# Three-layer attention block on one core: the second attention's probabilities in two layouts, with new waits and order at the start and around the third layer norm

## The chip, the cores and the metric

The kernel runs on one core of a Trainium2 chip and is written in Bass, with a program of its own for each engine: TensorE (PE; its weight loads are listed as PEld), VectorE (DVE), ScalarE (ACT), GpSimd (POOL) and SyncE (SP, which only issues DMAs here). The engines run side by side and meet at semaphores: `engine.wait_ge(sem, n)` holds an engine until the count is n, `.then_inc(sem, 1)` raises it. Each engine takes its instructions in the order in which they are written. The metric is the time on the device in microseconds (us). Of the kernel before there are three timed runs, 743.19, 739.35 and 742.94 us (median 742.94), and one profiled execution of 739.54 us.

## The reference

Everything is float32. Three residual layers act on x (4 batches of 128 rows, 512 wide, 16 heads of 32).

```
x = x + cross_attention(layernorm(x), ctx)   # ctx (4, 2048, 512); softmax over the 16*4 head-batch axis
x = x + relative_attention(layernorm(x))     # logits and values also take tables of relative distances:
#   attn = softmax((q.k + q.Ek[rel] + k.Eq[rel] + Eq[rel].Ek[rel]) / sqrt(32))
#   out[b,h,l] = sum_m attn[b,h,l,m] v[b,h,m] + sum_m attn[b,h,l,m] Ev[rel[l,m]]
x = x + third_attention(layernorm(x))        # normalised queries, learned offset and temperature,
#   softmax, gates by a softmax with top 3 of 15, output projection
```

The last sum of the second layer is the *table product* of this text. Ev[rel[l,m]] depends on the query row l, so each of the 128 rows l has a matrix (128 keys x 32) of its own, and is multiplied with the 64 probability columns (16 heads x 4 batches) of that row.

## The kernel before

**Start.** SP loads x in one DMA of 1 MB (`load(x_res[:], x_rows, "x_in")`), then Wq, the bias columns, Wk, the first context tile and the rest. DVE waits for x, takes mean and variance of batch after batch (L1329, L1331), ACT takes the square root (L894; an activation table is loaded first) and DVE writes the normalised rows (L1338). PE transposes them (L363), with two small products between the batches whose result is not used (`keep_warm`, L524). ACT splits the transposed rows and Wq into a high part (casts, L967 and L957); the low part comes from DVE (L1355, L1359). The query projection (L538, L543) starts when all four high parts of x and both halves of Wq's are there.

**First attention** (to about 546 us): 16 context tiles, a loop that this change does not touch.

**Second attention** (about 565 to 660 us), in four head groups u of 4 heads. `relative(n)` makes the table terms of the logits in 16 pieces, which SP stores to DRAM (`rel_scratch`) and loads back with shifted rows (`rel_load`); `logits(u)` (PE, L655 and L660) adds the products; `add2(u)` (DVE, L1512) adds the other table term; `softmax2(u)` takes the maximum and subtracts it (L1516, L1518); `exp2(u)` is on ACT (L1093), for u = 3 in 16 activations of one head and batch each (L1099, released in two halves by `softmax2_last`, L1523 to L1529). `total2(u)` sums over the keys (DVE, L1533). `attention_t(u)` transposes the probabilities on PE (L681) into PSUM; `at_copy(u)` (ACT, L1113) brings them into `blocks`, for u = 2 DVE does it (L1562). `blocks` holds, for a key in each partition, [u, batch, head, query row l]. `values2(b)` projects the values (L391), `attend2(u)` multiplies probabilities and values (L715) for one head group. The table product (L745) is 128 products of `ev_rel[:, l, :]` (128 keys x 32, the stationary operand) with

```
blocks[:, :, :, l].rearrange("p (u b) j -> p b u j", u=C)     # 64 columns, 512 bytes apart
```

in four PSUM banks of 8 x 4; between bank 0 and bank 1, PE transposes the attended values (`attended_t`, L733), and DVE scales them and adds x (L1573, L1575). An fp32 product with a plain weight shows as two records in the trace, so the table product has 256 records.

**Third layer norm** (about 655 to 675 us): DVE transposes the table product (L1581), POOL scales it by the inverse sums (L1311), PE adds it to PSUM (`table_values`, L762), DVE, ACT and PE do the norm and its transposes, `queries3(b)` projects (L391).

What sets the order is the text of each engine's program alone: no scheduler and no planner is in between. PSUM has eight banks (`ps[:, n, :]`), and who uses which is given by OUT_BANKS, THIRD_BANKS, LN_BANKS and the bank arguments.

Of the kernel before, what the change touches and what calls it, by code (L numbers as in the profile page):

```python
# [12 lines left out]
P = 128  # L13
B = 4
# [23 lines left out]
def program(nc, a, out):  # L38

    with ExitStack() as ctx:  # L40
# [102 lines left out]
        THIRD_BANKS = (7, 5, 6, 4)  # L143
# [13 lines left out]
        def ln_bank(k, b):  # L157
            return (4 + b, LN_BANKS[b], (4, 5, 6, 4)[b])[k]
# [70 lines left out]
        def probs_t(u):  # L229
            return blocks[:, u * B:(u + 1) * B]  # L230

        names = """x_in wq_in wk_in wv_in cols_in bv_in bo_in tab_in ctx_in_0 ctx_in_1 ctx_hi ctx_lo wq_split xq_split wkv_hi wkv_lo wraw_in wodd_in wsplit_hi wsplit_lo wo_lo wq2_lo
# [5 lines left out]
            ev_in kf_evac kr_evac qr_evac q2_psum q2_evac k2_psum v2_psum v2_evac rel_psum rq_evac rk_evac  # L238
# [3 lines left out]
            at_psum at_done at_dve av2 av2_evac av2_t av2_mul av2_done ev2 ev_t ev_mul x2_psum x2_done  # L242
# [3 lines left out]
            lg3_psum max3 sub3 exp3 sum3 rinv3 rexp3 rb_psum ot3_done at3_psum at3_done av3 ot3_evac ot3_hi ot3_lo  # L246
            g_psum g_bias g_max g_sub g_exp g_top g_steps y_psum fin_done out_done""".split()
# [15 lines left out]
        def _(sp):  # L263
# [3 lines left out]
            x_rows = a["x"].rearrange("b q e -> q b e")  # L267
            load(x_res[:], x_rows, "x_in")
# [82 lines left out]
        def _(pe):  # L351
# [284 lines left out]
            def values2(b, bank):  # L636
                if b == 0:
                    weight_ready(3)
                if b == 0:
                    pe.wait_ge(s["rk_evac"], 2 * C)  # L640
                else:
                    pe.wait_ge(s["at_done"], (2, B + 1, B + 2)[b - 1])
# [21 lines left out]
            def attention_t(u):  # L664
                base = 0 if u < 2 else 4
# [4 lines left out]
                elif u == 2:  # L670
                    pe.wait_ge(s["lg_done"], C + 1)
                for b in range(B):
                    if u == 1:
                        pe.wait_ge(s["at_done"], b + 1)
                        if b == 1:
                            pe.wait_ge(s["v2_evac"], 2)
                    if u == C - 1:
                        pe.wait_ge(s["at_dve"], b + 1)
# [26 lines left out]
            values2(2, 0)  # L705
            values2(3, 1)
            logits(3)

            def attend2(hg):
                for b in range(B):  # L710
                    if hg == C - 1:
                        pe.wait_ge(s["at_done"], 2 * B + b + 1)
# [24 lines left out]
            pe.wait_ge(s["ev_in"], 16)  # L737
            for bank in range(4):
# [1028 lines left out]
```

## Time and profile before

| | |
|---|---|
| timed runs, us | 743.19, 739.35, 742.94 (median 742.94) |
| profiled execution | 739.54 us; span from the first to the last instruction 737.3 us |
| PE | 710.5 us busy (96% of the span), granted clock 0.998 on the mean |
| DVE | 630.1 us (85%) |
| ACT, POOL | 488.9 us (66%), 501.6 us (68%) |
| DMA | 55.70 MB, mean 76 GB/s |

The busy times overlap, since the engines work side by side. An engine near 100% is the likeliest bound of its stretch, but a short stretch can hang on a chain through several engines. In a row of the timeline the first number is the start in us, the second the length, "xN" the number of instructions merged in it, and the bracket the idle time before it and what ended it. For neighbouring instructions the length of a group is more to be trusted than the duration of one, since they overlap in the engine.

### The profile page before, as it was taken

How to read it: one execution, taken by the hardware profiler on the slowest of the kernel's cores; microseconds unless marked ns; L12 is line 12 of the kernel's file. 1: busy time of each engine (PE TensorE's matmuls, PEld its weight loads, DVE VectorE, ACT ScalarE, POOL GpSimd, SP SyncE). 2: the span in 40 equal slices, each digit the busy share in tenths (PEclk: the TensorE clock that was granted, in tenths of full speed). 3: DMA queues.
4: the chain of work that ended last, by engine and by line, in shares of the span. 5: the costliest groups of instructions: out<-in, count | busy, mean ns of one | idle time of the engine just before them, and what ended most of it. 6: DMA issues, size and time to landing. Idle time of an engine off the chain costs nothing.

```text
span 737.3 us, 17280 instructions
## 1 busy us (share of the span) xinstructions
PE 710.5 (96%) x7530; PEld 565.4 (77%) x7530; DVE 630.1 (85%) x515; ACT 488.9 (66%) x693; POOL 501.6 (68%) x283
## 2 busy tenths in 40 slices
PE   8999999999999999999999999999989999889988
PEld 7777778777777777778777787777767667768776
DVE  5479999999999999899999999999986458886785
ACT  4569677686777768677686777768643446635681
POOL 0155979899898988989898898987993020064300
PEclk9999999999999999999999999999999999999999
DMA  8310110101011010110101011010002899621101
GB/s 338 114 59 2 58 48 12 59 2 58 2 59 58 2 59 1 59 35 25 59 1 59 1 59 59 1 59 2 1 12 96 283 392 374 240 101 58 58 2 57
DMA packets 15338, 55.70 MB, mean 76 GB/s; under 512 B 1696, under 2 KB 2080, under 8 KB 11680
## 3 DMA queue, kind: packets, MB, share of 16 engines
q1 hardware_dynamic: 15264, 54.61, 20.3%
q8 instruction: 59, 0.97, 0.6%
q14 instruction: 15, 0.12, 0.1%
HBM read 43.13 MB, written 11.47 MB: 74 GB/s over the span
## 4 chain that ended last, share of the span: by engine, by line
PE 80%; DVE 12%; ACT 5%; issue 3%; POOL 0%; ACTq 0%; DVEq 0%; POOLq 0%
PE ps L391 25%; PE ps L372 25%; PE ps L487 9%; PE ps L514 7%; PE ps L380 2%; PE ps L632 2%; PE ps L436 2%; DVE blocks L1502 1%; PE ps L745 1%; ACT v_buf L927 1%; DVE extra L1399 1%; DVE extra L1428 1%; DVE ps L1428 1%; PE ps L538 1%; PE ps L405 1%
## 5 line engine op out<-in xcount | busy, mean ns | idle before, releaser
L1263 POOL TENSOR_TENSOR s_buf<-s_buf,r_all 128x1024 f32<-128x1024 f32 x93 | 197.2, 2165 | 3.6 <-DVE r_all L1441 3.6
L951 ACT ACTIVATE s_buf<-s_buf 128x1024 f32<-128x1024 f32 x128 | 135.8, 1066 | 9.8 <-DVE s_buf L1421 9.0
L935 ACT COPY s_buf<-ps 128x1024 f32<-128x1024 f32 x128 | 123.4, 1018 | 20.4 <-PE ps L487 20.4
L1399 DVE TENSOR_REDUCE extra<-s_buf 128x128 f32<-128x2048 f32 x48 | 109.5, 2280 | 10.5 <-ACT s_buf L935 10.5
L1421 DVE TENSOR_TENSOR s_buf<-s_buf,ps 128x2048 f32<-128x2048 f32 x48 | 106.9, 2282 | 0.5
L927 ACT COPY v_buf<-ps 128x512 f32<-128x512 f32 x64 | 37.6, 587 | 77.6 <-PE ps L391 58.1
L1230 POOL TENSOR_TENSOR v_buf<-v_buf,extra 128x512 f32<-128x512 f32 x64 | 81.2, 1316 | 7.9 <-ACT v_buf L927 7.9
L1428 DVE TENSOR_REDUCE ps<-s_buf 128x128 f32<-128x4096 f32 x16 | 70.8, 4427 | 16.2 <-ACT s_buf L951 16.2
L1241 POOL TENSOR_TENSOR w_lo<-raw,w_hi 128x2048 fp32r<-128x2048 f32 x5 | 23.1, 4615 | 84.9 <-ACT w_hi L902 84.9
L1236 POOL TENSOR_TENSOR odd_lo<-extra,odd_hi 128x512 fp32r<-128x512 f32 x32 | 41.0, 1306 | 56.2 <-ACT odd_hi L910 56.2
L487 PE MATMUL ps<-q_t,k_t 32*128 32x128 f32 x2048 | 75.1, 283 | 2.3 <-ACT k_t L917 0.2
L487 PEld LDWEIGHTS ps<-q_t,k_t 32*128 32x128 f32 x2048 | 63.3, 186 | 17.7 <-issue 17.7
L514 PE MATMUL ps<-s_buf,v_buf 128*32 128x128 f32 x2048 | 71.8, 279 | 2.5 <-DVE s_buf L1449 2.5
L514 PEld LDWEIGHTS ps<-s_buf,v_buf 128*32 128x32 f32 x2048 | 54.3, 108 | 25.6 <-issue 25.6
L1428 DVE TENSOR_REDUCE extra<-s_buf 128x128 f32<-128x2048 f32 x32 | 72.9, 2277 | 0.0
L1257 POOL TENSOR_TENSOR s_buf<-s_buf,m_all 128x2048 f32<-128x2048 f32 x16 | 66.2, 4139 | 2.7 <-DVE m_all L1414 2.7
L917 ACT ACTIVATE k_t<-ps,cols 128x512 f32<-128x512 f32 x64 | 44.2, 691 | 28.1 <-PE ps L372 27.3
L1236 POOL TENSOR_TENSOR x_lo<-raw,x_hi 128x512 fp32r<-128x512 f32 x28 | 35.8, 1306 | 18.4 <-ACT x_hi L910 18.4
L391 PE MATMUL ps<-w_hi,x_hi 128*128 128x512 f32 x176 | 48.1, 395 | 0.0
L391 PE MATMUL ps<-w_lo,x_hi 128*128 128x512 f32 x176 | 47.1, 389 | 0.0
L391 PE MATMUL ps<-w_hi,x_lo 128*128 128x512 f32 x176 | 47.0, 389 | 0.0
L1399 DVE TENSOR_REDUCE ps<-s_buf 128x128 f32<-128x2048 f32 x16 | 36.7, 2296 | 9.7 <-ACT s_buf L935 8.1
(222 smaller groups left out, 1448.0 us busy)
## 6 DMA issues: line engine op xcount, KB each, us to landing
rel_scratch<-blocks SPq DMA_DIRECT2D x16, 636.0 KB, 10.9
s_buf<-rel_scratch SPq DMA_DIRECT2D x7, 1210.0 KB, 9.7
raw<-in_ctxT SPq DMA_DIRECT2D x8, 1024.0 KB, 4.9
extra<-in_ctxT SPq DMA_DIRECT2D x8, 1024.0 KB, 4.9
raw<-in_Wq SPq DMA_DIRECT2D x2, 1024.0 KB, 6.5
raw<-in_Wv SPq DMA_DIRECT2D x2, 1024.0 KB, 4.8
extra<-in_EvRel SPq DMA_DIRECT2D x1, 2048.0 KB, 13.8
extra<-rel_scratch SPq DMA_DIRECT2D x1, 1210.0 KB, 9.6
```

The lines of the kernel that those rows point to most:

```text
L372: last = mm(ps[:, bank, :], w_parts[v][:, slot, c, hg * P:(hg + 1) * P], x_parts[u][:, c, :], start=n + c == 0, stop=n == 2 and c == C - 1)
L391: last = mm(ps[:, bank, :], x_parts[u][:, c, b * P:(b + 1) * P], w_parts[v][:, slot, c, :], start=n + c == 0, stop=n == 2 and c == C - 1)
L487: last = mm(pair, k_t[rows, w, keys], q_t[rows, w, keys], start=True, stop=True, skip_group_check=True)
L514: last = mm(ps[j * HD:(j + 1) * HD, bank, b * P:(b + 1) * P], v_of(t)[:, b, h * HD:(h + 1) * HD], probs[:, j, b // 2, :, b % 2], start=b = ...
L935: copy(piece(t, 2 * w + u).rearrange("p e (u n) -> p (e u) n", u=2), ps[:, 2 * u:2 * u + 2, :]).then_inc(s["s_evac"], 1)
L951: nc.scalar.activation(piece(t, p), piece(t, p), ACT.Exp).then_inc(s["exp_done"], 1)
L1230: pool.tensor_tensor(v, v, bv_all, ALU.add).then_inc(s["v_ready"], 1)
L1236: pool.tensor_tensor(lo[:, :, rows], raw_of(t)[:, :, rows], hi[:, :, rows], ALU.subtract).then_inc(s["ctx_lo"], 1)
L1263: pool.tensor_tensor(part, part, spread(r_all, 4), ALU.mult).then_inc(s["attn_pool"], 1)
L1399: nc.vector.tensor_reduce(m_ps if k == 0 else m_next[:, k % 2, :], over_pairs(t, 2 * k, 2), AX.XY, ALU.max).then_inc(s["max_done"], 1)
L1421: tt(part, part, m_wide.broadcast_to([P, 8, P, 2]), ALU.subtract).then_inc(s["sub_dve"], 1)
L1428: nc.vector.tensor_reduce(r_ps if k == 0 else z_next[:, k % 2, :], over_pairs(t, p, n), AX.XY, ALU.add).then_inc(s["sum_done"], 1)
```

## The change

**Start.** x comes in four DMAs of 256 KB with a semaphore each, and the moments of a batch wait for that batch alone. A square root on one column is put first on ACT, so that the table load comes before x. The four square roots stand ahead of all casts. Half of Wq's cast moves to POOL.

**Second attention, order.** `attention_t(2)` moves up, behind `logits(3)` and ahead of `values2(3)`, uses banks 0 to 3 like u = 0 and 1, and its copy is ACT's. `logits(3)` moves ahead of `values2(3)`. `attention_t(3)` comes in two halves around `attend2(0)` and `attend2(1)`. DVE copies the last values into SBUF instead of ACT. The sum of u = 3 is taken by ACT with its exponentials (`accum_out`), and `total2(3)` goes.

**Second attention, two layouts.** `blocks` stays as it is for `attend2`. Beside it stands a copy in which the 16 probabilities of one row l, head group and all batches lie together (`probs_l`): POOL copies u = 0, 1, 2 out of `blocks`, DVE copies u = 3 out of PSUM. The table product reads this copy, four pieces of 16 columns (`probs_row`).

**Third layer norm.** DVE scales the first batch of the table product itself. PE does 12 and 5 small products with a zero matrix between (`add_zeros`), and the transposes of the next batch stand inside `queries3(b)`. Banks are given out anew, and some semaphores are joined.

```diff
+        def probs_l(u):
+            at = (0, 1, C, C + 1)[u] * B * ROWS
+            return flat[:, at:at + H * P].rearrange("p (l b j) -> p b j l", b=B, j=J)
+        def probs_row(l):
+            return flat[:, 0:6 * B * ROWS].rearrange("p (h o r) -> p h o r", h=3, o=2)[:, 0:3:2, :, l * H:l * H + H]
...
-            load(x_res[:], x_rows, "x_in")
+            for b in range(B):
+                load(x_res[:, b, :], a["x"][b], f"x_in_{b}")
... PE
+            logits(3)
+            attention_t(2)
             values2(3, 1)
-            logits(3)
-            pe.wait_ge(s["v2_evac"], B)
-            pe.wait_ge(s["at_done"], 2 * B)
+            attention_t(3, range(2))
+            pe.wait_ge(s["at_done"], 3 * B)
+            pe.wait_ge(s["v2_dve"], 1)
             attend2(0)
             attend2(1)
-            attention_t(2)
-            attention_t(3)
-            pe.wait_ge(s["at_dve"], B)
+            attention_t(3, range(2, B))
             attend2(2)
             attend2(3)
...
             pe.wait_ge(s["ev_in"], 16)
+            pe.wait_ge(s["rows_pool"], C - 1)
+            pe.wait_ge(s["rows_dve"], B)
...
-                                  blocks[:, :, :, l].rearrange("p (u b) j -> p b u j", u=C), start=n == 0, stop=n == 7,
+                                  probs_row(l), start=n == 0, stop=n == 7,
...
+            def add_zeros(n):
+                for _ in range(n):
+                    mm(ps[:, B - 1, 0:P], m_all[:], ident[:], start=False, stop=False, skip_group_check=True)
+            pe.wait_ge(s["zero_done"], 1)
+            pe.wait_ge(s["av2_done"], B)
+            add_zeros(12)
+            table_values(0)
+            add_zeros(5)
+            table_values(1)
+            table_values(2)
... ACT
             act.wait_ge(s["eps_done"], 1)
+            nc.scalar.activation(gtmp[:, 1, 7:8], eps, ACT.Sqrt).then_inc(s["eps_done"], 1)
+            act.wait_ge(s["eps_done"], 2)
+            for b in range(B):
+                ln_std(0, b)
...
-                                                    bias=rmax[:, u * H + n:u * H + n + 1])
+                                                    bias=rmax[:, u * H + n:u * H + n + 1],
+                                                    accum_out=rsum[:, u * H + n:u * H + n + 1])
... POOL
+            pool.wait_ge(s["wq_in"], 16)
+            pool.tensor_copy(wq_hi[:, 2:4], wq_raw[:, 2:4]).then_inc(s["wq_split"], 1)
...
+            pool.memset(m_all[:], 0.0).then_inc(s["zero_done"], 1)
+            def rows(u):
+                pool.wait_ge(s["at_done"], B * (u + 1))
+                if u < 2:
+                    pool.wait_ge(s["sum2"], u + 1)
+                else:
+                    pool.wait_ge(s["lg_psum"], C)
+                pool.tensor_copy(probs_l(u), probs_t(u)).then_inc(s["rows_pool"], 1)
+            for u in range(C - 1):
+                rows(u)
             pool.wait_ge(s["sub2"], C + 1)
             weight_lo(4)
... DVE
-            slot_landed(dve, 3, 4)
-            for b in range(B):
-                dve.wait_ge(s["at_psum"], 2 * B + b + 1)
-                nc.vector.tensor_copy(probs_t(2)[:, b],
-                                      ps[:, 4 + b, :].rearrange("p (j l) -> p j l", j=J)).then_inc(s["at_dve"], 1)
-            for u in range(1, C):
-                total2(u)
-            dve.wait_ge(s["sum2"], C)
+            dve.wait_ge(s["v2_psum"], B)
+            nc.vector.tensor_copy(v_buf[:, 1, B - 1, :], ps[:, 1, :]).then_inc(s["v2_dve"], 1)
+            total2(2)
+            for b in range(B):
+                dve.wait_ge(s["at_done"], 3 * B + b + 1)
+                nc.vector.tensor_copy(probs_l(C - 1)[:, b],
+                                      ps[:, 4 + b, :].rearrange("p (j l) -> p j l", j=J)).then_inc(s["rows_dve"], 1)
+            dve.wait_ge(s["sum2"], C - 1)
+            dve.wait_ge(s["exp2"], C - 1 + B)
```

Order on ACT at the start, before. "gtmp" is the epsilon of the norm, "mean_var" the moments, "xq_hi" and "wq_hi" the high parts of x and Wq.

```order
1 L894 ACT_TABLE_LOAD
2 L894 ACTIVATE rstd<-mean_var,gtmp 128x1 x2
3 L957 CAST wq_hi<-s_buf 128x1024
4 L894 ACTIVATE rstd<-mean_var,gtmp 128x1
5 L957 CAST wq_hi<-s_buf 128x1024
6 L894 ACTIVATE rstd<-mean_var,gtmp 128x1
7 L967 CAST xq_hi<-ps 128x4x128 x4
```

The same place on ACT now:

```order
1 L978 ACT_TABLE_LOAD
2 L978 ACTIVATE gtmp<-gtmp 128x1
3 L918 ACTIVATE rstd<-mean_var,gtmp 128x1 x4
4 L987 CAST xq_hi<-ps 128x4x128
5 L985 CAST wq_hi<-s_buf 128x1024
6 L987 CAST xq_hi<-ps 128x4x128 x3
```

The table load has a square root of its own that waits for no x, the roots stand together, and one of the two casts of Wq is gone from ACT.

Order on PE at the end of the second attention, before: "x_hi" and "w_hi" rows are the last values, 655 and 660 are `logits(3)`, 681 the transposes of probabilities, 715 `attend2`, 745 the table product.

```order
640 L391 MATMUL ps<-w_hi,x_hi 128x512 x4
641 L391 MATMUL ps<-w_lo,x_hi 128x512 x4
642 L391 MATMUL ps<-w_hi,x_lo 128x512 x4
643 L655 MATMUL ps<-ident,s_buf 128x128 x16
644 L660 MATMUL ps<-v_buf,s_buf 128x128 x16
645 L715 MATMUL ps<-blocks,v_buf 32x128 x32
646 L681 MATMUL ps<-ident,s_buf 128x128 x32
647 L715 MATMUL ps<-blocks,v_buf 32x128 x32
648 L745 MATMUL ps<-blocks,extra 32x64 x32
649 L733 MATMUL ps<-ident,k_t 128x128 x16
650 L745 MATMUL ps<-blocks,extra 32x64 x96
651 L762 MATMUL ps<-v_buf,ident 128x512 x4
```

The same place on PE now (the rows of the changed kernel have its own line numbers):

```order
640 L662 MATMUL ps<-ident,s_buf 128x128 x16
641 L667 MATMUL ps<-v_buf,s_buf 128x128 x16
642 L689 MATMUL ps<-ident,s_buf 128x128 x16
643 L398 MATMUL ps<-w_hi,x_hi 128x512 x4
646 L689 MATMUL ps<-ident,s_buf 128x128 x8
647 L724 MATMUL ps<-blocks,v_buf 32x128 x32
648 L689 MATMUL ps<-ident,s_buf 128x128 x8
649 L724 MATMUL ps<-blocks,v_buf 32x128 x32
650 L755 MATMUL ps<-s_buf,extra 32x64 x32
652 L755 MATMUL ps<-s_buf,extra 32x64 x96
653 L786 MATMUL ps<-ident,m_all 128x128 x12
654 L780 MATMUL ps<-v_buf,ident 128x512
```

The last logits and the transposes of group 2 stand ahead of the last values, the transposes of group 3 are halved, the table product reads s_buf (the copy), and 12 products with zeros stand ahead of the first L780.

Order on DVE at the end of the second attention, before (1562 copies group 2, 1533 are sums):

```order
350 L1529 TENSOR_SCALAR rmax<-rmax 128x8
351 L1562 COPY blocks<-ps 128x512 x4
352 L1533 TENSOR_REDUCE rsum<-s_buf 128x16 x3
353 L1567 RECIPROCAL rinv<-rsum 128x64
354 L1573 TENSOR_TENSOR ps<-ps,rinv 128x512
```

The same place on DVE now:

```order
351 L1561 TENSOR_SCALAR rmax<-rmax 128x8
352 L1596 COPY v_buf<-ps 128x512
353 L1565 TENSOR_REDUCE rsum<-s_buf 128x16
354 L1600 COPY s_buf<-ps 128x4x128 x4
355 L1604 RECIPROCAL rinv<-rsum 128x64
```

Three sums have become one, the four copies now belong to group 3 and write the second layout, and the last values are copied here.

## Rows read from the trace of the kernel before

**Rows 1.** The page: share of the last-ending chain by engine.

```profile
PE 80%; DVE 12%; ACT 5%; issue 3%; POOL 0%; ACTq 0%; DVEq 0%; POOLq 0%
```

**Rows 2.** Timeline of the start: start us, length us, engine, line, what.

```profile
1.52 6.75 PE L524 MATMUL ps<-ident 128*128 128x128 f32 x44 [1.52 <-POOL ident L1220]
...
6.32 0.69 DVE L1329 BATCH_NORM_STATS2 stats<-x_res 128x6 f32<-128x512 f32 x1 [6.32 <-issue]
...
7.31 1.28 ACT L894 ACT_TABLE_LOAD   x1 [7.31 <-DVE mean_var L1331]
...
8.99 1.03 ACT L957 CAST wq_hi<-s_buf 128x1024 fp32r<-128x1024 f32 x1
9.13 0.55 DVE L1338 TENSOR_SCALAR v_buf<-x_res,mean_var,rstd 128x512 f32<-128x512 f32 x1
...
15.37 0.59 ACT L967 CAST xq_hi<-ps 128x512 fp32r<-128x512 f32 x1 [1.00 <-PE ps L363]
...
16.01 3.93 PE L538 MATMUL ps<-xq_hi,wq_hi 128*128 128x512 f32 x16 [0.23 <-ACT xq_hi L967]
```

**Rows 3.** Windows of the start: window, length, busy PE to POOL, PEclk, DMA, GB/s.

```profile
8.30:9.70 1.40, 0.00 (x0) 0.00 (x0) 0.73 (x3) 1.39 (x4) 0.00 (x0) 1.00 1.06 441
...
11.50:14.50 3.00, 3.00 (x17) 2.81 (x15) 2.89 (x7) 2.11 (x5) 0.00 (x0) 0.53 1.04 404
```

**Rows 4.** Timeline of the second attention, DVE, SP, PE and ACT.

```profile
618.72 7.11 SPq L265 DMA_DIRECT2D s_buf<-rel_scratch  x2
...
622.18 2.29 DVE L1512 TENSOR_TENSOR s_buf<-ps,s_buf 128x2048 f32<-128x2048 f32 x1 [3.11 <-DMA s_buf<-rel_scratch]
...
630.12 1.91 PE L655 MATMUL ps<-ident,s_buf 128*128 128x128 f32 x16
...
633.20 1.23 DVE L1523 TENSOR_TENSOR s_buf<-ps,s_buf 128x1024 f32<-128x1024 f32 x1 [1.88 <-PE ps L660]
...
635.92 5.04 ACT L1099 ACTIVATE s_buf<-s_buf,rmax 128x128 f32<-128x128 f32 x16 [2.08 <-DVE rmax L1529]
...
638.41 2.48 DVE L1562 COPY blocks<-ps 128x512 f32<-128x512 f32 x4
...
640.86 2.00 ACT L1113 COPY blocks<-ps 128x512 f32<-128x512 f32 x4
```

**Rows 5.** DMA view of 622 to 628 us: issue, engine, count, size, us to landing.

```profile
s_buf<-rel_scratch SPq DMA_DIRECT2D x1, 1210.0 KB, 6.2
```

**Rows 6.** Line 1176 (activations that also sum, third attention): start and length.

```profile
693.44 0.29 ACT L1176 ACTIVATE s_buf<-s_buf 128x128 f32<-128x128 f32 x1
693.64 0.19 ACT L1176 ACTIVATION_READ_ACCUMULATOR s_buf<-s_buf 128x1 f32 x1
693.74 0.29 ACT L1176 ACTIVATE s_buf<-s_buf 128x128 f32<-128x128 f32 x1
```

**Rows 7.** Timeline: attend2, the table product's first bank and the rest.

```profile
641.66 1.96 PE L715 MATMUL ps<-blocks,v_buf 128*32 128x128 f32 x64
...
643.43 2.51 PE L745 MATMUL ps<-blocks,extra 128*32 128x64 f32 x64
...
647.77 7.20 PE L745 MATMUL ps<-blocks,extra 128*32 128x64 f32 x192
```

**Rows 8.** Groups of instructions: copies with and without spread writes; GpSimd, 2048 wide.

```profile
L1072 ACT COPY v_buf<-ps 128x512 f32<-128x512 f32 x4 | 4.3, 1071 | 3.7 <-PE ps L380 3.7
...
L1060 ACT COPY x_res<-ps 128x512 f32<-128x512 f32 x3 | 1.8, 589 | 2.2 <-DVE v_buf L1338 2.2
...
L1241 POOL TENSOR_TENSOR w_lo<-extra,w_hi 128x2048 fp32r<-128x2048 f32 x1 | 4.6, 4600 | 0.0
...
L1302 POOL CAST w_hi<-raw 128x2048 fp32r<-128x2048 f32 x1 | 1.9, 1892 | 6.5 <-PE ps L405 6.5
```

**Rows 9.** Timeline around the third layer norm.

```profile
657.07 4.11 PE L762 MATMUL ps<-v_buf,ident 128*128 128x512 f32 x8 [2.11 <-POOL v_buf L1311]
...
662.56 1.17 PE L391 MATMUL ps<-w_hi,x_hi 128*128 128x512 f32 x4
```

More of the change, by code:

```diff
@@ L662, in logits, with attention_t @@
                 last.then_inc(s["lg_psum"], 1)
-            def attention_t(u):
-                base = 0 if u < 2 else 4
+            def attention_t(u, batches=range(B)):
+                base = 0 if u < C - 1 else 4
                 if u < C - 1:
@@ L752, in queries3 @@
                     weight_ready(4)
-                if b == 0:
-                    pe.wait_ge(s["x_hi_done"], 3 * C + 1)
-                else:
-                    pe.wait_ge(s["x_lo_done"], 2 * C + b + 1)
-                proj_n(0, THIRD_BANKS[b], s["q3_psum"], b, low_ready=("x_lo_done", 2 * C + 1) if b == 0 else None)
+                for n, (u, v) in enumerate(PARTS):
+                    if n == 0:
+                        pe.wait_ge(s["x_hi_done"], 3 * C + b + 1)
+                    if n == 2:
+                        if b + 1 < B:
+                            if b + 1 == B - 1:
+                                pe.wait_ge(s["x2_done"], 1)
+                            transposes(y_ln, 2, b + 1)
+                        pe.wait_ge(s["x_lo_done"], 2 * C + b + 1)
+                    for c in range(C):
+                        last = mm(ps[:, THIRD_BANKS[b], :], x_parts[u][:, c, b * P:(b + 1) * P], w_parts[v][:, 0, c, :],
+                                  start=n + c == 0, stop=n == 2 and c == C - 1, skip_group_check=True)
+                last.then_inc(s["q3_psum"], 1)
             def table_values(b):
@@ L1132, in _ @@
             exp2(2)
-            values2(3, 1)
+            at_copy(2)
             exp2(3)
@@ L1308, in _ @@
             pool.wait_ge(s["rinv2"], 1)
-            for b in range(B):
+            pool.wait_ge(s["ev_mul"], 1)
+            for b in range(1, B):
                 pool.wait_ge(s["ev_t"], b + 1)
@@ L1345, in split_lo, with moments0 @@
                    ALU.subtract).then_inc(s["x_lo_done"], 1)
-            dve.wait_ge(s["x_in"], 16)
             nc.vector.memset(eps, EPS).then_inc(s["eps_done"], 1)
-            for b in range(B):
+            def moments0(b):
+                dve.wait_ge(s[f"x_in_{b}"], 16)
                 moments(0, b)
-                if b >= 1:
-                    normalised(0, b - 1)
-            normalised(0, B - 1)
+            moments0(0)
+            moments0(1)
+            normalised(0, 0)
+            moments0(2)
+            normalised(0, 1)
+            moments0(3)
+            normalised(0, 2)
+            normalised(0, 3)
             dve.wait_ge(s["wq_split"], 2)
@@ L1550, in _ @@
                     query_rows(hg)
-            for u in range(C - 1):
-                add2(u)
-                softmax2(u)
+            add2(0)
+            softmax2(0)
+            add2(1)
+            softmax2(1)
             total2(0)
+            add2(2)
+            softmax2(2)
+            total2(1)
             dve.wait_ge(s["lg_psum"], C)
@@ L1586, in moments2 @@
                 moments(2, b)
-            for b in range(B):
-                ev_transpose(b)
+            ev_transpose(0)
+            dve.wait_ge(s["ev_t"], 1)
+            tt(by_head(ev_rows[:, 0, :]), by_head(ev_rows[:, 0, :]), per_head(rinv, 0), ALU.mult).then_inc(s["ev_mul"], 1)
+            ev_transpose(1)
+            ev_transpose(2)
             moments2(0)
-            moments2(1)
+            ev_transpose(3)
             normalised(2, 0)
-            normalised(2, 1)
-            moments2(2)
-            split_lo(2, 0)
-            normalised(2, 2)
-            split_lo(2, 1)
-            moments2(3)
-            normalised(2, 3)
-            split_lo(2, 2)
-            split_lo(2, 3)
+            for b in range(1, B):
+                moments2(b)
+                split_lo(2, b - 1)
+                normalised(2, b)
+            split_lo(2, B - 1)
             def bias_q3(b):
```

104 lines of the change are left out of this document (40 added, 64 removed).

## The prediction

> **What bounds the kernel now.** I read the chain of work first: PE holds 80% of it, DVE 12% [rows 1]. Almost every microsecond that PE waits or works less at the ends is therefore a microsecond of the kernel, and one saved on DVE, ACT or POOL is worth something only where PE waits for it. The reader is to look for PE's waits at the three places that change.
>
> Start, by its timeline: DVE begins at 6.32 us, when all of x is there; the table load of the square root comes after it (7.31, 1.28 us long) and holds up the first normalised rows to 9.13 + 0.55; the first query product starts at 16.01, behind the fourth high part of x (15.37 + 0.59) [rows 2]. PE was idle from 8.30 to 9.70, and from 11.50 to 14.50 its granted clock was 0.53, about the 1.2 GHz level [rows 3].
>
> Second attention: DVE waits 3.11 us for a load from DRAM until 622.18, the last logits are done on PE at 633.2, and everything hangs on them: DVE's add at 633.20, the exponentials at 635.92, ACT's copies at 640.86 to 642.86 [rows 4], then attend2 and the table product to 654.97 [rows 7], then POOL's scaling, the norm and the last layer [rows 9].
>
> **Start: minus 3.9 us.** One x DMA landed at 6.32. In four pieces the same megabyte passes through the same queue, so the last should land at about 6.3 and the first about 2.5 us earlier. The table load lies before all this, at no cost. Last batch: moments 0.87 (statistics 0.69 [rows 2] and their aggregation, about 0.2), root 0.3, reciprocal 0.15, rows 0.55, with DVE shared among batches: about 9.9. PE is then the later one: its 22 idle products end at 8.27 (1.52 + 6.75) [rows 2] and without the 1.40 us gap I expect the full clock. Four times transposes 0.44 and two idle products 0.44 give the fourth transposes at 8.27 + 3 x 0.88 + 0.44 = 11.35. ACT: batch 0 at about 9.4, its half of Wq 1.03 (Wq landed by 8.99 [rows 2]; POOL does the other half in about half of 1.89, rows 8), then three copies of 0.59 in step with PE: 12.1. The query projection starts at 12.1 instead of 16.01. Behind it DVE's low part of Wq (2.29, from 10.4) and ACT's cast of Wk have as much lead as before. The three added DMA issues of 0.45 us delay Wq's issue from 1.2 to 2.7, but it queues behind x's data anyway. If the clock stays low or the pieces land late, this is 1.2 rather than 3.9; I take 3.9.
>
> From here all of the first attention is earlier by one amount; I write the times of before and subtract it at the end.
>
> **Logits of group 3: minus 1.4.** total2(0) falls into DVE's 3.11 us wait, free. On PE logits(3) moves ahead of a projection of 2.75 us, from 630.1 to 627.4, but its table terms come with the load issued at 618.72, which takes 9.6 like its neighbours: 628.3. The last load of all is issued at about 625.5 [rows 4] and takes 6.2 [rows 5]: 631.7. DVE's add waits for it and starts at 631.75 instead of 633.20. So what is late next is a DMA, and half of the gain of the new order goes to it.
>
> **Exponentials: plus 1.5.** They start at 634.5. Without a sum they have a pitch of 0.31 (5.04 / 16 [rows 4]). With a sum and without a bias the pitch is 0.30, of which 0.09 to 0.1 is the read of the accumulator [rows 6]; bias and sum together occur nowhere. Bounds: 0.31 (the read is hidden) and 0.50 (0.31 and the whole read of 0.19 behind it, which would end them at 642.5). I take 0.31 + 0.09 = 0.40, as in rows 6, where the read overlaps half: 6.4 us, end 640.9, the same as before. ACT's four copies end at 643.0. The moved transposes, the last values (until 636.1) and attend2(0), (1) (until 639.7) stand before that on PE. attend2(3) ends at about 643.3, where before it was 643.4.
>
> **The second layout: plus 0.8.** POOL's three copies of 2048 elements: a cast costs 1.89, a two-input instruction 4.6 [rows 8]. Both write in sequence; these write with a step of 64 bytes. ACT's copy with spread writes costs 1.07 against 0.59 [rows 8], a factor 1.8; I take 1.89 x 1.8 = 3.4, range 1.9 to 4.6. rows(0) starts at 621.4, rows(1) after total2(1) at 631.4, rows(2) after that: ends at 638.2 (641 at 4.6). That is hidden under ACT's exponentials. weight_lo(4) is queued behind it, but it waits for ACT until 645 anyway. DVE's four copies start at 641.5 after ACT's first copy and end, one every 0.62 (2.48 / 4 [rows 4]), bounded by ACT's last at 643.0 plus 0.65 and a queue of three: 644.1. With the factor 1.8 (1.1 each) it would be 645.9. I take 0.62, the same operation on the same engine, keeping both. PE starts the table product at 644.1 instead of 643.4, since now all copies must be there, not only the last transposes.
>
> Here a rule of the Trainium skill speaks against the change: "SBUF — State Buffer", section Door 1, says that SBUF is read and written in lines of 16 bytes and that every access that goes to a new line pays. ACT's 1.07 against 0.59 agrees. By that rule the copies pay for what the product saves: both would sit at the slow end (645.9), which is the second rival below.
>
> **The table product: minus 2.8.** 256 records take 2.51 + 7.20 = 9.7 us, 37.9 ns each, 64 columns. attend2 takes 64 records in 1.96: 30.6 ns each, with 128 columns and the same weight size [rows 7]. So with half the columns it is slower by a quarter; the difference in form is the step of 512 bytes between columns. With pieces of 16 in sequence I expect 27 ns a record (attend2's 1.96 less the overhang of its last record, about 0.25, over 64), 6.9 us. Bounds: 15 (half of attend2's, if columns were all that counts) and 37.9 (no help). I choose 27, since a record has a weight load, and attend2's is no shorter. The Trainium skill, "TensorE: Matmul & The Clock Gate", section "Wait — 56ns, not 53.3ns?", gives about 25 ns as the least from start to start of a matmul; by it the product would be 6.4 us and the bound of 15 out of reach.
>
> With the transposes between the banks (1.94) it ends at 644.1 + 1.94 + 6.9 = 653.0 instead of 655.0. DVE's eight scalings (5.4 us from about 646.5) end at 651.9, just hidden.
>
> **Third layer norm: plus 0.8.** Let E be the end of the table product. Before, the first table addition came at E + 2.1 and the first projection at E + 7.6 [rows 9]. Now DVE scales batch 0 itself and has it at E + 1.5, but PE first does 12 zero products: 22 idle ones took 6.75 with part at half clock, 0.22 each at full: 2.6. So the addition comes at E + 2.6. Five more (1.1), two additions, the third transpose on DVE behind the moments: normalised rows at E + 6.3, projection at E + 7.9. Three transposes of 0.44 now stand inside the projections, before two: 0.4 more. Also the root's table load on ACT ends at 657.9 whatever E is, up to 0.3. Together 0.5 to 1.0; I take 0.8. The granted clock here was not low before, so the zeros have nothing to give back.
>
> **Sum.** -3.9 at the start; E from 655.0 to 653.0 (-1.4 + 1.5 + 0.7 - 2.8) is -2.0; +0.8. In all -5.1 us. The profiled execution took 739.54 (2.2 outside the span of 737.3), so 734.4. Two of three timed runs are 3.4 to 3.6 higher; halfway between profile and median (741.2), less 5.1, is 736.1. I say 736.
>
> **Rivals.** Gains against before, then the time on the same level.
> - *The spread writes cost 1.8 times on DVE*: the product starts at 645.9, the gain of the second attention falls from 2.0 to 0.3. In all 3.4, 738. For it: ACT's rows. Against: DVE is slower per element than ACT and may hide it.
> - *The product isn't bound by the step* between columns but by something else in it: 9.7 us as before, E at 655.7 and all else kept. In all 2.4, 739. For it: the trace shows no such product without the step. Against: attend2 has the same weight shape, twice the columns and less time a record [rows 7].
> - *The start gives only 1.2*: the clock falls anyway, or x's pieces land late. In all 2.4, 739.
> - *Slower: GpSimd's copies gate the product.* PE waits for rows_pool. If one takes R, the third is done at 631.4 + 2R; the end of the product is this plus 8.8. R decides from 6.4 on; at R = 9 all gains are gone, at 11 the kernel is 4 us slower, 745. For it: POOL is the slowest on 2048 elements (4.6) and no row shows it writing with a step. Against: it would need 5 times the cast's time.
>
> **Chances.** Forecast 0.55 (own range 734 to 739), spread writes 0.17, product not helped 0.10, start 0.12, GpSimd 0.06. A measurement of this kernel can't tell less than about 0.5% (3.7 us) from no change, which is 739.2 against the median. Faster by more: 0.5 of the forecast's 0.55, 0.12 of the second, 0.03 each of the next two: 0.68. Slower: 0.05. Within: 0.27. The range of 8 in 10 is 732 to 741: below, the bound of 15 ns (3 us less) in part; above, the gains of 2.4 from the median's level (740.5).
>
> **What would show it.** L538's counterpart starts at 12 (start right) or 14 to 16 (wrong), with a granted clock of 1.00 before it. DVE's first add of group 3 comes 1.4 earlier, released by a DMA. The summing exponentials have a pitch of 0.40. POOL's copies take 1.9 to 4.6. PE's wait before the table product ends on DVE, not POOL, and is under 1.5 us; its records come every 27 ns. The first projection comes 7.9 after the product's end. Wrong would be a wait on POOL before the product, or a new wait in the untouched last layer.

## The result and the profile after

The changed kernel takes 743.73 us (median of 22 runs, 741.08 to 746.51), the kernel before, beside it, 741.46 us (22 runs). The ratio is 1.004 with a 95% interval of 1.0029 to 1.0052: 0.4% slower, where 736 and a range of 732 to 741 were forecast. The profiled execution took 744.49 us, span 742.6 us.

On the page, PE's part of the chain is smaller than before [rows 1], and a DMA has come in:

```profile
PE 75%; DVE 10%; DMA 6%; ACT 6%; issue 2%; POOL 1%; SPq 0%; ACTq 0%; POOLq 0%; DVEq 0%
```

The timeline of the start answers to [rows 2]: the first query product is at 12.03 instead of 16.01.

```profile
9.09 1.04 POOL L1236 CAST wq_hi<-s_buf 128x1024 fp32r<-128x1024 f32 x1 [7.62 <-DMA s_buf<-in_Wq]
...
12.03 3.92 PE L545 MATMUL ps<-xq_hi,wq_hi 128*128 128x512 f32 x16 [0.23 <-ACT xq_hi L987]
```

The second attention in the timeline, answering to [rows 4] and [rows 7]:

```profile
621.94 3.79 POOL L1326 COPY s_buf<-blocks 128x2048 f32<-128x2048 f32 x1 [12.51 <-DVE rsum L1565]
...
632.49 7.32 POOL L1326 COPY s_buf<-blocks 128x2048 f32<-128x2048 f32 x2 [6.76 <-DVE rsum L1565]
632.79 1.23 DVE L1555 TENSOR_TENSOR s_buf<-ps,s_buf 128x1024 f32<-128x1024 f32 x1 [0.43 <-DMA s_buf<-rel_scratch]
...
635.31 4.52 DVE L1561 TENSOR_SCALAR rmax<-rmax 128x8 f32<-128x8 f32 x1
...
639.87 0.40 ACT L1117 ACTIVATE s_buf<-s_buf,rmax 128x128 f32<-128x128 f32 x1 [4.61 <-DVE rmax L1561]
640.17 0.19 ACT L1117 ACTIVATION_READ_ACCUMULATOR s_buf<-s_buf,rmax 128x1 f32 x1
640.27 0.39 ACT L1117 ACTIVATE s_buf<-s_buf,rmax 128x128 f32<-128x128 f32 x1
...
644.15 3.10 PE L724 MATMUL ps<-blocks,v_buf 128*32 128x128 f32 x64
...
650.59 1.10 PE L755 MATMUL ps<-s_buf,extra 128*32 128x64 f32 x64 [0.43 <-DVE s_buf L1600]
...
653.51 2.54 PE L755 MATMUL ps<-s_buf,extra 128*32 128x64 f32 x164
```

The reader is to see the third of DVE's rows here. It scales 8 maxima per partition, which takes 0.17 us a few rows on, and it takes 4.52 us. It ends at 639.83, and GpSimd's two copies in a row end at 632.49 + 7.32 = 639.81. By its row the next addition (L1555) starts at 636.07, where GpSimd's first copy ends, and lasts to 639.83 as well, so both stand to the end of the second copy. The exponentials wait 4.61 us for the maxima, PE stands still for 4.30 us behind them, and its granted clock falls to the 1.2 GHz level (windows; the columns are those of [rows 3]):

```profile
637.00:641.00 4.00, 0.36 (x2) 0.00 (x0) 3.94 (x3) 1.13 (x6) 2.81 (x1) 0.84 0.36 152
641.00:645.00 4.00, 2.98 (x24) 2.22 (x28) 3.07 (x4) 4.00 (x23) 0.00 (x0) 0.50 0.02 4
```

attend2's first 64 records then take 3.10 us instead of 1.96. Once PE gets there, the table product runs at 2.54 us / 164 = 15.5 ns a record, against 37.9 before. A group's row gives its busy us, the mean ns of one and the idle time before it. Two such rows show what the product costs and what its operand costs DVE:

```profile
L755 PE MATMUL ps<-s_buf,extra 128*32 128x64 f32 x256 | 4.3, 220 | 1.5 <-issue 1.0 <-DVE s_buf L1600 0.4
...
L1600 DVE COPY s_buf<-ps 128x512 f32<-128x512 f32 x4 | 3.8, 1044 | 2.5 <-ACT blocks L1127 2.5
```

At the third norm, answering to [rows 9], the first projection is at 666.55 instead of 662.56, and DVE's first bias addition (L1641) at 676.77 instead of 670.48, right behind DVE's last low part:

```profile
660.46 1.90 ACT L926 CAST w_hi<-raw 128x2048 fp32r<-128x2048 f32 x1 [7.76 <-DMA raw<-in_Wk]
660.74 1.02 PE L780 MATMUL ps<-v_buf,ident 128*128 128x512 f32 x2
662.38 1.28 ACT L918 ACT_TABLE_LOAD   x1
...
666.55 1.16 PE L773 MATMUL ps<-w_hi,x_hi 128*128 128x512 f32 x4
...
676.16 0.69 DVE L1369 TENSOR_TENSOR x_lo<-ps,x_hi 128x512 fp32r<-128x512 f32 x1 [1.61 <-ACT x_hi L1063]
...
676.77 1.28 DVE L1641 TENSOR_TENSOR s_buf<-ps,extra 128x512 f32<-128x512 f32 x2
```

**Time and granted clock.** Every run lists its mean granted clock, and with it the time goes in steps. Of 35 executions of the kernel before in one series, 5 had 1.000 and took 738.1 to 738.4 us, 7 had 0.998 (739.3 to 740.0), 19 had 0.995 (740.8 to 741.5), 3 had 0.993 (742.4 to 742.5) and one 0.991 (743.7). A step is about 1.35 us, what one stretch of some 3 us at half clock costs. The kernel before averages 0.996, the changed one 0.990 (22 executions, 0.986 to 0.993): two to three such stretches more, some 3 us of time. At the same mean clock the two kernels take the same: at 0.993 the changed one 741.1 to 743.0 us (7 executions), the one before 742.1 to 742.9 (24 executions of all series). This doesn't make the clock the only loss. The changed kernel never ran above 0.993, and the experiments show that a gain at the start and a loss in the second attention stand against each other in it.

Where does the clock fall? In the trace of the changed kernel windows of 4 us with less than 0.95 start at 80, 84, 544, 564, 640 and 644 us, in that of before only at 12. Ahead of the falls at 80 to 88, 544 and 564 PE stands still, and it does so in the trace of before too. Two of these gaps in the changed kernel, then the same two in the kernel before:

```profile
82.93 1.74 PE L398 MATMUL ps<-w_hi,odd_hi 128*128 128x512 f32 x4 [1.81 <-ACT s_buf L959]
...
563.18 0.66 PE L370 MATMUL ps<-ident,v_buf 128*128 128x128 f32 x4 [1.07 <-DVE v_buf L1363]
```

```profile
86.90 1.19 PE L391 MATMUL ps<-w_hi,odd_hi 128*128 128x512 f32 x4 [1.78 <-ACT s_buf L935]
...
564.23 0.66 PE L363 MATMUL ps<-ident,v_buf 128*128 128x128 f32 x4 [1.07 <-DVE v_buf L1338]
```

In the changed kernel the clock is 0.50 soon after each of these gaps, in the kernel before it is 1.00. So a gap alone doesn't bring the fall.

### The profile page after: what moved, and what is told of

The parts are those of the page before. It is cut to its first block, busy times and chain, and to the rows that moved or that the text cites. A ratio compares the mean times of both kernels' runs of the same rounds, so it can differ in the third digit from the quotient of the medians.

```text
span 742.6 us, 17379 instructions
## 1 busy us (share of the span) xinstructions
PE 713.1 (96%) x7564; PEld 566.7 (76%) x7564; DVE 634.8 (85%) x516; ACT 491.5 (66%) x712; POOL 512.9 (69%) x287
## 4 chain that ended last, share of the span: by engine, by line
PE 75%; DVE 10%; DMA 6%; ACT 6%; issue 2%; POOL 1%; SPq 0%; ACTq 0%; POOLq 0%; DVEq 0%
PE ps L379 24%; PE ps L398 22%; PE ps L494 9%; PE ps L521 7%; DMA rel_scratch<-blocks 4%; PE ps L443 2%; PE ps L387 1%; ACT v_buf L951 1%; DVE extra L1431 1%; DVE extra L1460 1%; DVE ps L1460 1%; PE ps L412 1%; PE ps L531 1%; PE ps L773 1%; PE ps L545 1%
## 5 line engine op out<-in xcount | busy, mean ns | idle before, releaser
L398 PE MATMUL ps<-w_hi,x_hi 128*128 128x512 f32 x160 | 43.6, 394 | 0.0
L379 PE MATMUL ps<-x_hi,w_hi 128*128 128x512 f32 x144 | 42.5, 417 | 0.3
L398 PE MATMUL ps<-w_lo,x_hi 128*128 128x512 f32 x160 | 42.8, 389 | 0.0
```

The source lines that it names most:

```text
L379: last = mm(ps[:, bank, :], w_parts[v][:, slot, c, hg * P:(hg + 1) * P], x_parts[u][:, c, :], start=n + c == 0, stop=n == 2 and c == C - 1)
L398: last = mm(ps[:, bank, :], x_parts[u][:, c, b * P:(b + 1) * P], w_parts[v][:, slot, c, :], start=n + c == 0, stop=n == 2 and c == C - 1)
```

## Experiments

All have 12 timed executions beside before, where nothing else is said, and were taken in several series. Differences are of medians. By the spread of the executions a difference between two kernels is known to about 1 to 2 us only, and it is given with that margin where it matters.

**1. The start changes alone** (before, with x in four loads, the early root, POOL's cast and DVE's order; the diff is the start's part of the change).

> The kernel before with the start changes alone (x in four loads, the early root, the half cast on GpSimd, the order on DVE). All theories: the first query product starts at 12.0 instead of 16.0. Theory 1 (the gain is real and reaches the end; the stretches at the lower granted clock in the trace of after come from the second attention's changes or from chance): the ratio to before is 0.995 (3.7 to 4.0 us less), and the first table product of the second stage, 502 us in, is 3.9 us earlier. Theory 2 (starting earlier itself moves idle gaps of PE so that the granted clock falls in the first attention): this kernel shows the same stretches below 1.00 near 76 to 96, 541 to 549 and 561 to 569 us, and gains only 0 to 2.6 us.

739.54 against 740.82 (0.9986, 0.9972 to 1.0), mean clock 0.994. A repeat in another series:

> A repeat of the kernel before with the start changes alone, run beside the next one for their clocks. Expected of all theories: 739.5 us and a mean clock of 0.994.

740.04 against 739.92, by the means 739.4 against 740.7 (0.9977, 0.9959 to 0.9996), clock 0.995. Timeline of the first run:

```profile
10.62 1.04 POOL L1222 CAST wq_hi<-s_buf 128x1024 fp32r<-128x1024 f32 x1 [9.16 <-DMA s_buf<-in_Wq]
...
13.41 2.79 PE L538 MATMUL ps<-xq_hi,wq_hi 128*128 128x512 f32 x11 [0.23 <-ACT xq_hi L963]
```

Two things take the gain. Wq's DMA lands at 8.4 to 10.6 in the traces of these kernels, so the query product is at 12.0 to 13.4, 2.6 to 4.0 us earlier. And the clock falls later on, which PE's trace of before doesn't show in any place behind the start. Windows of run 1, near 544 and 656 us:

```profile
544.00:548.00 4.00, 4.00 (x46) 2.94 (x50) 1.83 (x3) 0.00 (x0) 4.00 (x3) 0.62 0.00 0
...
656.00:660.00 4.00, 4.00 (x6) 1.52 (x6) 2.01 (x6) 0.87 (x3) 4.00 (x4) 0.57 0.23 94
```

The repeat fell near 84, 544 and 564 us instead, each time behind a gap of PE. Among executions with the same mean clock this kernel is 1.1 to 2.7 us faster than before. Theory 2 holds as far as the size goes; that it is the earlier start that brings the falls was then put to three tests (9, 11 and 13).

**2. GpSimd's copies late.**

```
 def rows(u):
     pool.wait_ge(s["at_done"], B * (u + 1))
+    if u == 1:
+        pool.wait_ge(s["sub2"], C + 1)
```

> The changed kernel, GpSimd's second and third layout copies held back until VectorE has scaled the maxima of the last group. Theory (a GpSimd copy under way blocks VectorE's 128x8 scaling of the maxima): that instruction takes 0.2 instead of 4.52 us, ScalarE's last exponentials start at 635.5 instead of 639.9, the table product starts 3 to 4 us earlier (GpSimd's last copy ends at about 643.5 and is hidden), and the kernel is 3 to 4.5 us faster than the changed one (739.5 to 740.5). Rival (VectorE waited for something else, such as the write of the maxima or a DMA): the instruction still takes over 4 us and the time stays at 743.7.

739.21 us, 4.5 less than the changed kernel (4.7 by the means, give or take 1.5), clock 0.995. Timeline:

```profile
631.45 0.17 DVE L1563 TENSOR_SCALAR rmax<-rmax 128x8 f32<-128x8 f32 x1
...
634.33 7.43 POOL L1328 COPY s_buf<-blocks 128x2048 f32<-128x2048 f32 x2 [12.32 <-DVE rmax L1563]
...
642.38 1.10 PE L755 MATMUL ps<-s_buf,extra 128*32 128x64 f32 x64 [1.86 <-DVE s_buf L1602]
...
653.40 1.90 ACT L926 CAST w_hi<-raw 128x2048 fp32r<-128x2048 f32 x1 [9.85 <-DMA raw<-in_Wk]
...
655.32 1.28 ACT L918 ACT_TABLE_LOAD   x1
656.62 0.29 ACT L918 ACTIVATE rstd<-mean_var,gtmp 128x1 f32<-128x1 f32 x1
...
659.49 1.17 PE L773 MATMUL ps<-w_hi,x_hi 128*128 128x512 f32 x4
```

The scaling takes 0.17 us and in this execution PE's clock is 1.00 all through. The theory holds: what held VectorE was the copies under way, since the instruction, its input and its place are the same. The rest of the rows show the next floor: ACT's cast of the sixth weight stands ahead of the first root in ACT's order and waits 9.85 us for a DMA.

**3. Bias additions early** (after, `bias_q3(0)` and `bias_q3(1)` ahead of `split_lo(2, B - 1)`).

> The changed kernel with VectorE's two first bias additions of the third queries ahead of its last low part. Theory (in the changed order they wait behind the last low part, which waits for the last high part): the first bias addition is at about 674.6 instead of 676.8, the queries are normalised 0.7 to 1.0 us earlier after the last projection, 742.9. Rival (the chain behind the last projection sets the time whatever stands before): no difference at the end, 743.7.

742.95 us, 0.8 less, as expected, but known to 1.1 us only. The trace shows the mechanism: the first bias addition starts 7.9 us after the first projection (664.65 and 672.57), as in the kernel before, and 10.2 in the changed one.

**4. One layout** (after, without the seven copies, product on `blocks[:, :, :, l]` again).

> The changed kernel without the second layout: the seven copies are left out and the table product reads the probabilities with the step of 512 bytes, as before. Theory (the copies cost 4.4 us by the block and 4 us by standing between the transposes and the product; the product gains 5.4 of which VectorE's scalings hide 3): VectorE's scaling of the maxima takes 0.2, the product starts at about 644.5 and takes 9.7 us without the transposes between, end of the product 656 instead of 654.9, VectorE's scalings hidden; the kernel takes 741 to 742. Rival (the second layout is worth having even so, since the product is so much faster): 745 or more.

741.75 us, and the scaling takes 0.17, as expected. Beside experiment 2 (means 740.8 and 739.0 in one series), the second layout is worth 1.7 us once its copies hold nobody, give or take 1.9, so this gain isn't clear of noise. As it was built it lost 2.0 (3.0 by the means, give or take 1.5).

**5. Two inputs for the scaling.**

```
-nc.vector.tensor_scalar(top, top, -SCALE, None, ALU.mult)
+tt(top, top, gtmp[:, 2, 7:8].broadcast_to([P, 8]), ALU.mult)
```

> The changed kernel, with VectorE's scaling of the last maxima (SBUF to SBUF, one input and a constant) written as a product of two inputs (the maxima and a constant column); GpSimd's copies run beside it as in the changed kernel. Theory 1 (only the one-input form on SBUF is held by a GpSimd instruction that is under way): the scaling takes 0.2 instead of 4.52 us although GpSimd copies at the same time, the exponentials start 4.3 us earlier than in the changed kernel, and the time is that of the kernel with the late copies, 739.2, or 0.3 less. Rival (any VectorE instruction that starts there is held by GpSimd's copy): it takes 4 us again, 743.7.

739.55 us, so the time is that of theory 1. The rows are not quite:

```profile
634.03 7.38 POOL L1326 COPY s_buf<-blocks 128x2048 f32<-128x2048 f32 x2 [6.47 <-DVE rsum L1567]
...
636.83 0.86 DVE L1563 TENSOR_TENSOR rmax<-rmax,gtmp 128x8 f32<-128x8 f32 x1
```

This form was held too (0.86, and 1.16 for the second), and the first one only until the copy under way ended, at 634.03 + 3.69 = 637.72. The one-input form of the changed kernel was held through two copies.

**6. Roots and bias additions early** (experiments 2 and 3, and on ACT `weight_hi(5)` from ahead of the norm to behind `residual2(0)`).

> The changed kernel with late copies, the early bias additions, and ScalarE's third norm roots (with their table load) ahead of its cast of the sixth weight. Theory (with the block gone, the cast that waits for Wk3's DMA until 653.4 and the table load behind it hold the first root until 656.6 instead of 654.5, so the third norm costs 9.9 us from the end of the second attention to the first projection instead of the 7.6 of before): first projection about 2 us earlier than with late copies alone, first bias addition not behind the last low part, in all 2.5 to 3 us less than that kernel's 739.2, so 736.5. Rival (the low part of the sixth weight comes later and stops the keys of the last stage): PE waits before the first keys of the last stage, and the time is 739 or more.

737.01 us (0.9962, 0.9939 to 0.9984), 2.2 less than with late copies alone (1.3 by the means, give or take 2). ACT's first root now follows the moments at once. Its profiled execution, 741.1, shows something else:

```profile
653.79 0.64 PE L755 MATMUL ps<-s_buf,extra 128*32 128x64 f32 x28 [4.07 <-issue]
```

PE stood 4.07 us in the middle of the product with nothing to wait for that the profile shows, and DVE's first transpose waited 4.49 us for it. In the changed kernel this gap is 1.02, in experiment 2 1.05. The kernel's lowest time is 734.5.

**7. Without the zero products.**

> The kernel of the run above without the 12 and 5 zero products ahead of the first two table additions. Theory 1 (the zeros stand in the way: PE works on them until 1.5 us after the first scaled rows are ready): the first projection is 1.0 to 1.5 us earlier, 735.3. Theory 2 (the zeros keep PE's clock up): PE's granted clock falls to 0.5 near 655 to 665 us, the projections there take up to twice as long, and the kernel is 1 to 2 us slower than with them.

737.94 us; the means of this and the kernel with the zeros are the same (737.8), the mean clocks 0.9925 and 0.9955. Windows:

```profile
652.00:656.00 4.00, 3.79 (x5) 1.45 (x6) 2.92 (x8) 0.29 (x1) 2.17 (x3) 0.50 0.40 164
656.00:660.00 4.00, 4.00 (x12) 2.02 (x11) 2.24 (x5) 1.37 (x4) 0.93 (x1) 0.70 0.01 4
```

The clock falls as theory 2 has it, and 0.003 of it is 1.7 us at 5.5 us for 0.01; the time stays, so leaving the zeros out would have to save about that. The fall of theory 2 is in the trace. The saving of theory 1 is only inferred from the times: from the product's end to the first projection it is 8.8 us here, with half clock in it, and 9.4 in experiment 6, whose trace has half clock there too.

**8. Transposes ahead of the product** (experiment 6, and on PE all `attended_t(b)` before the product, on ACT the copies for them before `weight_hi(4)`, 5 zeros for 12). 6 executions.

> The kernel with late copies, early bias additions and early roots (737.0 us), with PE's transposes of the attended rows ahead of the table product instead of behind its first bank, ScalarE's copies for them ahead of its cast of the fifth weight, and 5 instead of 12 zero products. Theory (PE waits for VectorE's layout copies from 640.2 to 642.4, so these transposes are free there; VectorE's scalings, which end last, start 2 us earlier, and the zeros end with the scaled rows): the scalings end at 647.6 instead of 649.6, the first projection comes 3 us earlier, 734. Rival (the 256 products in one row are then held by PE's instruction supply, which shows as gaps of 1 to 4 us without a wait in the product): the product ends at 648.5 or later, and the time is 735.5 or more.

734.06 us (0.9903, 0.9886 to 0.992), the best here: 1% below before, 9.7 us below the changed kernel (of another series). The first projection is at 655.71.

```profile
643.66 3.43 PE L754 MATMUL ps<-s_buf,extra 128*32 128x64 f32 x228
...
648.24 0.64 PE L754 MATMUL ps<-s_buf,extra 128*32 128x64 f32 x28 [1.15 <-issue]
```

The gap without a wait is there again (the rival's mechanism), but hidden: DVE's scalings start with the product here and end at 649.07, the product ends at 648.88.

**9. The start changes with the query product 4 us later** (18 more idle products).

> The kernel before with the start changes, and 18 more idle products of 0.22 us on PE ahead of the first query product, so that everything behind it stands where it stands in the kernel before, but without the stretch at half clock in the start. Two earlier runs of the start changes alone gave 739.5 and 740.0 us at mean clocks of 0.994 and 0.995, against 0.996 of before. Theory 1 (how often the clock falls depends on when the work lies): the mean clock rises to 0.997 or more, and the time is only 1 to 2 us above those two, near 741 (before, which also loses a stretch in the start, is at 740.8). Theory 2 (each execution loses one to four stretches by chance, wherever the work lies): the clock stays at 0.994 to 0.995 and the time rises by the whole 4 us, to 743.5.

743.30 us, clock 0.995: theory 2. Where the work lies in time isn't it. The query product starts at 15.49 here, earlier than in the trace of before, and still the kernel is 2.3 us slower by the means: the 16.01 of before has a stretch at half clock ahead of it, and this kernel pays for its stretches later.

**10. The last kernel with the old start.** 6 executions.

> The last kernel of the series so far (transposes ahead of the table product, 734.1 us) with the start of the kernel before. Theory (the start changes are worth 1 to 1.5 us in the median, as in the two runs of them alone, whatever stands in the second attention): 735.2 to 735.8. Rival (in this kernel they keep their 3 to 4 us, since its clock, 0.997, is higher): 737 to 738.

735.10 us against 734.06: the start is worth 1.0 (1.2 by the means, give or take 1.1).

**11. A gap of PE in the start** (start changes, 15 idle products for 22, none between the transposes).

> The kernel before with the start changes, with 15 instead of 22 idle products on PE and none between the transposes, so that PE idles some 3 us near 6 to 9 us as it idled 1.4 us in the kernel before. Theory A (a stretch at half clock in the start, as before has it, is what keeps later ones away): the clock falls in the start, the later work shows at most one such stretch, the mean clock is 0.996 or more, and the time is 739 or less although the transposes in the start take twice as long. Theory B (the later stretches come whether or not the clock fell in the start): the mean clock is 0.992 to 0.994 and the time 740 to 741.5.

739.77 us, clock 0.994, half clock near 12, 544 and 564 us: theory B by its clock, 0.2 us under its range of times.

**12 and 13. Before, 2 us later; x in four loads alone** (8 executions).

> The kernel before with 9 more idle products of 0.22 us on PE ahead of the first query product, and nothing else. Theory 1 (where the long gaps of PE lie in time decides how often the clock falls): the mean clock drops to 0.994 or 0.995 and the time is 3 us or more above before. Theory 2 (a shift alone does nothing): mean clock 0.996, as before, and the time is 1.8 to 2.0 us above before.

> The kernel before with x in four loads and VectorE's order for them, without the early root and without the half cast on GpSimd. Theory 1 (the root's table load and ScalarE's two casts of Wq's halves then still hold the fourth high part): the first query product is 1 to 2 us earlier than before, and with the mean clock of the other start kernels (0.994 to 0.995) the time is that of before, 740 to 741. Theory 2 (the loads bring the whole gain, and the falls come from elsewhere): first query product at 12.0 to 13.4 us, mean clock 0.996, time 738.

743.51 against 741.09 (by the means 1.7 apart), and both at a clock of 0.995 in this series: a shift costs its own time and does nothing to the clock. Its profiled execution falls near 12, 548 and 660 us, so before's program, with nothing but idle products added, has these falls too. The four loads give 739.83 (0.9977, 0.9963 to 0.9992) at a clock of 0.996 with a query product at 14.88: as much as all start changes together.

## Why the prediction was wrong

**Start, -3.9.** The mechanism is right: 12.03, with full clock. What failed is "from here all of the first attention is earlier by one amount". In three comparisons (1, its repeat, 10) the start is worth 0.8 to 1.3 by the means. Of the 3.9, up to 1.4 goes where Wq lands late (query product at 12.0 to 13.4), which the one trace of before couldn't show. The rest goes to stretches of half clock. Over a whole execution they are 0.5 to 1.1 more than before has (mean clocks 0.0013 to 0.0026 apart in four series, 0.0024 a stretch). Three traces with the old start have one in the start, and that one is gone; so behind the start it is 1.5 to 2.1 more, an estimate of 2.0 to 2.8 us. They come by chance and at the same few gaps of PE. What makes them more frequent in the kernels with the start changes stays open: not the shift, not the full clock in the start, and the four loads alone have a mean clock no lower than before's in their series.

**Logits, -1.4.** Right, as far as experiment 2 shows it. There the exponentials start at 631.65 against 635.92, -4.3, of which 3.0 is the start.

**Exponentials, +1.5.** The pitch was right: 0.386 us against 0.40 forecast, 6.2 us for all.

**"That is hidden under ACT's exponentials": this step failed, and it cost most.** GpSimd's copies were sized well (3.7 us each, 3.4 forecast) and nobody waits for their output. I looked for who waits for them and not for whom they hold. Price by experiment 2: 4.5 us. In the traces the block itself is 4.35, and PE's idling behind it brings the half clock from 640 to 645, a stretch of 1.35 or more; of this experiment 2 gives 1.1 away at the third norm (first projection 9.9 us after the product's end instead of 8.8). None of the 22 executions of the changed kernel has a mean clock above 0.993. The Trainium skill, "SBUF — State Buffer", section "Who interferes with whom", states it: a tensor_scalar that works from SBUF to SBUF can take the port pair which VectorE shares with GpSimd, and whoever comes second stands until the other's instruction is done. The trace agrees as to the block (4.52 instead of 0.17). It states the same of two inputs in SBUF against a GpSimd that reads there, and experiment 5 agrees (0.86). That it lasts to the end of a second copy in a row is this case's, and why is open. The slower rival named the right engine, and a wrong path: it had PE wait for the copies, from 6.4 us each on.

**DVE's layout copies, 0.62 each.** 1.04: the rival of the spread writes was right on this, with a factor of 1.7 instead of 1.8. In experiment 2 PE waits 1.86 us for them.

**Product, -2.8.** Mis-sized to the good: 4.3 us plus the gap of 1.0, where 6.9 was forecast; 15.0 to 17.2 ns a record, at my lower bound. My 27 leant on attend2's 30.6 as a price of the weight load. With half the columns a record takes about half of that, so the load, which is the same, can't be what takes 30.6. The least of about 25 ns from start to start that the Trainium skill gives ("TensorE: Matmul & The Clock Gate", section "Wait — 56ns, not 53.3ns?") isn't what the trace shows: 15.5. Here four neighbouring products write four different groups of 32 rows; products that follow each other into the same rows were not measured. Little of it arrives: DVE's scalings behind the first bank and the gap end the second attention at 657.8 in the changed kernel. In experiment 8, where the scalings start with the product, the kernel is 3.0 us faster than in experiment 6.

**Third norm, +0.8.** The first projection comes 8.8 us after the product's end, where 7.9 was forecast and before had 7.6. Two terms were missing. First, "the root's table load ends at 657.9 whatever E is" was costed at 0.3. The load stands behind ACT's cast of the sixth weight, and that waits for a DMA, until 660.46 in the changed kernel, where the load ends at 663.66. It is a floor that a better second attention meets: in experiment 2 the first projection comes 9.9 us after its end instead of 7.6. Second, I didn't write down DVE's order: the bias additions stand behind the last low part, 0.8 by experiment 3. Both together are 2.2 us by the medians in experiment 6, 1.3 by the means.

**Sum.** Forecast -5.1; measured +2.3 (medians) to +2.8 (means). The start misses by 2.8, the block by 4.5, the bias order by 0.8: 8.1, where 7.4 to 7.9 are missed. Each of the three is known to a microsecond or so, and the product's surplus and the floor at the third norm are in none of them by name, so that the sum comes out this close is in part luck.

## What to carry to other kernels

Work put on an idle engine isn't free where it can hold the engine on the path: list what that engine runs in the same microseconds, above all tiny instructions that others wait for, and move the copy or change the form. A faster stage is worth what the next-latest thing leaves, so read all of them, in each engine's order of instructions, before the gain is booked. Where the clock comes in steps, take a change's worth from many executions: one trace shows a place that fell, not how often it falls.

## What the runs showed of the hardware

- A VectorE instruction of 0.17 us was held 4.5 us by GpSimd, through two copies of 3.66; in a two-input form 0.86 and 1.16.
- A product of 64 columns with 128x32 weights, four neighbours into four groups of 32 rows, runs at 15.0 to 17.2 ns a record from pieces of 16 in sequence and at 37.9 with a step of 512 bytes.
- At that rate PE meets gaps of 0.9 to 4.1 us in which it waits for nothing that the profile shows, always ahead of the last 28 records; what fills them, the supply of instructions or something else, wasn't tried.
- A permuted write costs VectorE 1.04 us for 512 elements a partition against 0.62 in sequence, and GpSimd 3.7 for 2048, where its cast in sequence takes 1.89.
- PE falls to half clock for some 3 us behind gaps (of 1.8 us before 82.9, of 1.1 and 0.7 us before 564.6 in the changed kernel), 1.35 us of time each. Behind the same gaps (1.8 and 1.1) the trace of before has full clock, and so has that of experiment 2. What decides it stays open.
